# Two engines' loops over the turns of a relational graph stage, written out as straight code

## What is computed

```python
h = maximum(_layernorm(x), 0.0)
x = x + L0(h, edge_index, W_in, b_in, W_out, b_out)   # three rounds of normalised neighbour sums
h = maximum(_layernorm(x), 0.0)
# L1, the relational layer:
W_rel = einsum('rb,bio->rio', w_comp, weight)         # 64 relations from 16 bases
h_all = einsum('ni,rio->nro', h, W_rel)
msg = h_all[src, etypes] * norm
agg = segment_sum(msg, dst, num_segments=3125)
x = x + relu(agg + h_bias + h @ loop_weight)
```

## Time and profile before

| | |
|---|---|
| median of 3 runs | 1128.37 us (1128.1 to 1135.03) |
| the profiled execution | 1126.62 us |
| its span, first to last instruction | 1125.0 us |
| busy: PE / DVE / POOL / ACT | 890.1 / 812.3 / 555.3 / 358.3 us |
| the dearest group by busy time | L569, the gathers: 392.7 us |
| TensorE's mean granted clock over the span | 0.812 |

### The profile page before, as it was taken

One profiled execution on the slowest core, in us unless ns is written; L12 is line 12 of the kernel. 1 busy time (PEld: TensorE's weight loads), 2 busy tenths in 40 slices (PEclk: granted clock), 3 DMA queues, 4 the chain that ended last, 5 costly groups with the idle time before them and its releaser, 6 DMA issues.

```text
span 1125.0 us, 27667 instructions
## 1 busy us (share of the span) xinstructions
PE 890.1 (79%) x5568; PEld 596.5 (53%) x5569; DVE 812.3 (72%) x2477; ACT 358.3 (32%) x706; POOL 555.3 (49%) x581
## 2 busy tenths in 40 slices
PE   4777777777677769999982888988888888887666
PEld 3622222222223349999971666766665666565434
DVE  7799999999975545544451768777777878888544
ACT  0402344555565530000131445353443332221000
POOL 4055555555420000000015777777777777777773
PEclk9565555555555559999995999999999999999878
DMA  5013444565532220001139211111111111111113
GB/s 134 5 54 86 99 107 118 123 130 129 120 88 78 70 53 1 2 2 29 37 96 318 60 49 50 48 49 49 50 51 49 51 49 52 51 51 52 49 52 86
DMA packets 86977, 79.46 MB, mean 71 GB/s; under 512 B 33772, under 2 KB 73757, under 8 KB 86797
## 3 DMA queue, kind: packets, MB, share of 16 engines
q0 software_dynamic: 39504, 41.84, 14.7%
q1 hardware_dynamic: 47420, 36.97, 12.4%
HBM read 50.02 MB, written 8.09 MB: 52 GB/s over the span
## 4 chain that ended last, share of the span: by engine, by line
PE 30%; DVE 22%; issue 14%; DMA 14%; DVEq 8%; POOL 7%; ACT 2%; SPq 1%; POOLq 0%; ACTq 0%
PE ps L1036 13%; DVE ohbuf L746 9%; PE ps L1104 8%; DMA CT<-h_dram,src_col 8%; POOL CT L569 7%; PE ps L962 5%; DVE CT L859 4%; DMA CT<-stage 4%; DVEq L862 2%; DVE CT L862 2%; DVE ohbuf L743 2%; PE ps L1084 2%; DVEq L112 2%; DVEq L859 1%; DMA CT<-x 1%
## 5 line engine op out<-in xcount | busy, mean ns | idle before, releaser
L569 POOL DMA_INDIRECT CT<-h_dram,src_col x391 | 392.7, 1004 | 127.0 <-issue 97.5
L1104 PE MATMUL ps<-CT 128*128 128x256 f32 x1180 | 312.8, 414 | 77.6 <-DVE CT L862 39.3
L962 PE MATMUL ps<-ohbuf 128*128 128x400 bf16 x590 | 246.1, 510 | 89.8 <-DVE ohbuf L746 56.0
L1104 PEld LDWEIGHTS ps<-CT 128*128 128x128 f32 x1180 | 207.5, 196 | 177.5 <-issue 159.4
L862 DVE SCALAR_TENSOR_TENSOR CT<-iota,dlP,CT 128x256 f32<-128x256 int16 x590 | 286.4, 485 | 5.8
L859 DVE COPY CT<-CT 128x128 f32 x590 | 138.2, 234 | 140.2 <-PE ps L1104 68.0
L746 DVE TENSOR_SCALAR ohbuf<-iota,keys 128x400 bf16<-128x400 int16 x590 | 205.1, 386 | 0.0
L962 PEld LDWEIGHTS ps<-ohbuf 128*128 128x128 bf16 x590 | 63.0, 107 | 253.4 <-issue 226.2
L1243 ACT COPY CT<-ps 128x256 f32<-128x256 f32 x200 | 77.6, 388 | 330.9 <-PE ps L1104 327.2
L1184 ACT CAST stage<-ps 128x800 bf16<-128x800 f32 x100 | 82.5, 825 | 188.1 <-PE ps L962 169.8
L743 DVE TENSOR_TENSOR ohbuf<-iota,keys 128x640 bf16<-128x640 int16 x118 | 96.2, 815 | 38.4 <-PE ps L962 38.1
(11 more groups left out here) (164 smaller groups left out, 529.1 us busy)
## 6 DMA issues: line engine op xcount, KB each, us to landing
CT<-stage SPq DMA_DIRECT2D x200, 100.0 KB, 3.4
u<-edge_type POOLq DMA_DIRECT2D x48, 256.0 KB, 10.5
CT<-h_dram,src_col POOLq DMA_INDIRECT x391, 2.6
coef_dram<-coef_out POOLq DMA_DIRECT2D x49, 64.0 KB, 7.9
CT<-coef_dram SPq DMA_DIRECT2D x1, 3048.0 KB, 11.1
out<-CT SPq DMA_DIRECT2D x4, 256.0 KB
ohbuf<-x SPq DMA_DIRECT2D x3, 320.0 KB, 4.2
x_dram<-ohbuf SPq DMA_DIRECT2D x3, 320.0 KB, 2.4
```

The costliest lines, as they stand in the source:

```text
L569: pool.indirect_dma_start(out=gring[:, (j + 1) % GRING, :], out_offset=None, in_=h2_dram, in_offset=bass.IndirectOffsetOnAxis(ap=src_col[: ...
L962: pe.matmul(ps[:, ds(counted.place(counts[u][0], RING), 1), 0:LO], ohA[:, u, :], ohB[:, u, :], start=False, stop=True, skip_group_check=Tr ...
L1104: pe.matmul(ps[:, ds(summed.place(counts[u][0], RING), 1), 0:WIN * BASES], gpair[:, u, :], kpair[:, u, :, :].rearrange("p b d -> p (b d)") ...
```

## The change

VectorE's loop over turns 1 to 57 and TensorE's over turns 0 to 57 become Python loops, so that each turn's code stands once in the program with its number as a constant. The two alignments ahead of the loops go with them. Nothing else changes: the same operations in the same order on every engine.

```diff
@@ VectorE @@
             operands(0, first=True)
             dve.wait_ge(ld_coefs, 16)
-            dve.addr_align(BLOCK, offset=0, max_nops=0)
-            with dve.Fori(1, TURNS - 1) as c:
+            for c in range(1, TURNS - 1):
                 operands(c)
@@ TensorE @@
-            pe.addr_align(BLOCK, offset=0, max_nops=0)
-            with pe.Fori(0, TURNS - 1) as c:
+            for c in range(TURNS - 1):
                 sum_pairs(c)
                 complete_groups()
```

## The result

The changed kernel takes 1113.8 us (four runs, 1113.6 to 1114.0) where the kernel before takes 1129.9 (1128.1 to 1135.0): a ratio of 0.985, 95% interval 0.9815 to 0.9885. It is faster by 1.5%. The forecast was 1123, the range reached down to 1105.

| term | before, us | forecast | after, us |
|---|---|---|---|
| to the first gather | 599.7 | 599.7 | 597.9 |
| 390 gather periods | 510.5 (1.309 each) | 505.5 | 499.2 (1.280 each) |
| last gather and tail to the span's end | 14.8 | 14.6 | 14.9 |
| span | 1125.0 | 1119.8 | 1112.0 |

A forecast was written before the change was run, and what follows sets the result against it. GpSimd's gathers were taken as the bound: the profiled 1126.6 us, less 5 for shorter gathers and 0.2 in the tail, plus 0 for code, gave 1121.4; with the runs' median 1.8 higher, 1123. Range 1105 to 1138.

The forecast's parts named there:

- What bounds the kernel: GpSimd's 391 gathers, one every 1.309 us, none waiting for anything; VectorE and TensorE only consume what they fetch.
- (a): VectorE's loop written out: 1.2 us a turn, 68 us of VectorE's time, none of it on the path.
- (b): TensorE's loop written out: about 0.45 us a turn, 26 us of TensorE's time, also off the path.
- (c): GpSimd's gathers after about 900 us: VectorE's scalar_tensor_tensor lengthens fewer; 11.4 us at stake, 5 us taken as saved.
- R2: Rival, faster: gathers come clear of VectorE altogether, gaining 23 us, to 1105 us; chance 0.09.
- R3: Rival, slower: VectorE's written-out step locks on the harmful distance, hitting every gather; +24 us, 1152 us; chance 0.08.
- (d): The tail after the last gather: TensorE's loop end just before it goes, 0.2 us saved.
- (e): Fetching the added straight code on VectorE and TensorE: 38 more packets for TensorE, at a cost of 0.
- R1: Rival, slower: code arrives late on TensorE; 1201 us, or 1131 if only jumps crossing a block stall; chance 0.09.
- the sign named in the prediction: Sign of a wrong forecast by late code: TensorE's idle time "issue" of over 1 us between turns.
- no shift of 0.09 us would help: By the port rule alone, VectorE's scalar_tensor_tensor starting 0.09 us sooner saves gathers nothing: term 0, time 1128.

The follow-up runs named there:

- f4_ahead: Changed kernel with three more sequencer instructions on VectorE ahead of each two pairs, from waits always met; 1136.3 us, 1.007 of before.
- f6_psum: Changed kernel with the scalar_tensor_tensor's row of 0 to 15 read from PSUM instead of SBUF in turns 1 to 57; 1103.0 us, 0.977 of before.
- c0_before: The kernel before, unchanged, run again for a profile; 1131.9 us in its one run.
- c1_after: The changed kernel, unchanged, run again; 1115.2 us, 0.988 of before.

## Why the prediction was right or wrong

**What bounds the kernel** was right: gather after gather, before and after, and none that waits. A change that takes work from two engines that aren't the bound gave 1.5%, and it came through the bound's own instruction.

**(a) and (b), the two loops.** Two pairs on VectorE were forecast to go from 1.44 to 1.26 us and went to 1.21; the idle time for tiles was forecast at 70 us or more and is 61.5, and the wait for TensorE, which was to shrink, went from 56.2 to 51.0. TensorE's 26 us were not measured by themselves. That these gains aren't on the path held. I said of (a) that nothing of it is on the path: as a count of VectorE's time that is so, but VectorE's step is what drags the gathers.

**(c), the gather itself,** is the term that was mis-sized: 5 us forecast, 11.3 us measured (510.5 - 499.2). Its parts don't add up either: "some 190 gathers" after 900 us are 163 by the earlier trace rows (116 + 47), which makes 9.8 us at stake in place of 11.4. The mechanism was half seen. Right were the culprit (a scalar_tensor_tensor that starts a little ahead of a gather), that 0.34 us ahead does no harm, and the 0.70 us distance (0.68). The step that failed is the sentence "Before 900 us the engines meet at no fixed distance and I leave 1.31 to 1.33 us as it is". They met at a fixed distance for rows of gathers there, 0.15 to 0.17 us, in step at 1.43 us, and this stretch gave the larger part, 8.9 us. Behind 900 us, where I had put all 5 us, 2.4 were gained, and I put them down to the distance inside two pairs, which f4_ahead shows not to be what decides. That the range holds the result owes more to R2's bound than to the working of this term.

**R3** (the lock settles on the harmful distance) had the right mechanism at the wrong kernel. I asked whether a written-out step of 1.26 us could lock to a gather of 1.25 and not whether the loop's 1.44 did already. As I read the three cases, a lock needs VectorE's step to lie above the gather's own period, 1.25 us, and below its longest, 1.23 + 0.30: 1.43 locks (before), 1.49 locks (f4_ahead), 1.21 doesn't.

**R2** (no gather is hit) didn't come about through the change; f6_psum brought it about by other means, with about the saving that was worked out for it: 23 us forecast, 24.8 measured against before, with the loops written out too.

**(d), the tail,** was forecast 0.2 us shorter and came out 0.1 longer, 14.9 against 14.8: nothing. TensorE's low clock begins sooner, as said (granted 0.94 from 900 to 1050 us in place of 1.00), at no visible cost.

**(e) and R1, the code,** were right: 38 packets were forecast for TensorE and 38 came, another 35 came in the second queue, and no gather waited for it. TensorE's idle time that is put down to nothing, ahead of the pairs' weight loads, went from 159 us (up to 3.0 at once) to 139 (up to 2.6), so no late code shows there either; the sign named in the prediction, over 1 us of it, was there before the change.

**The start.** The first gather was 1.8 us earlier, which no step had. c0_before has it at 600.3 and c1_after at 597.6, f4_ahead at 599.2; among kernels that are the same up to there this scatters by as much, so I count it neither for nor against.

The Trainium skill ("SBUF — State Buffer", section on the two separate sides) has VectorE's operations with two SBUF inputs hold the port that they share with GpSimd. With the runs in hand: that the second SBUF input is the means is borne out by f6_psum, where one input went to PSUM and the stretching ended. The prediction read the rule so that any overlap should block the whole gather, and found it against the rows. Read with the ends of the instructions, they agree with a lock. A lengthened gather ends 0.81 to 0.82 us behind the end of the scalar_tensor_tensor ahead of it, whatever the distance: by the earlier trace rows 1055.35 - 1054.54, by c0_before 727.41 - 726.60, by f4_ahead 762.23 - 761.42. Over the traces of before, after, c0_before, c1_after and f4_ahead this holds for 632 of the 653 gathers over 1.0 us. An undisturbed gather takes 0.944 us, so by an estimate from these two it needs what the engines share some 0.13 us after its start, and stands until the other instruction is done. A scalar_tensor_tensor of 0.48 us that starts 0.35 us ahead or earlier is done by then: that is why the one 0.34 us ahead cost 0.01 and the one 0.39 us ahead, still running, nothing. One that starts less than about 0.1 us ahead mostly comes second, and is itself made longer (0.52 in place of 0.48 at 760.74, 0.54 in the mean of the 20 in before that start 0.08 to 0.10 us ahead). So "no shift of 0.09 us would help" doesn't follow from a lock: a start that is 0.09 us earlier saves 0.09 us.

## What to carry to other kernels

An engine that isn't the bound can still set the bound's pace: look whether the bound's instruction has one duration or several, and what the other engine starts just ahead of the long ones. When two engines that share something run at nearly the same period, the one that is a little faster can be held at the slower one's, so a gain on the slower one shows, and slowing it a little costs: here 1.5% gained and 2% lost, though VectorE had idle time to spare. To see the hold, compare the ends of the two instructions, not only their starts. The lasting cure is to take away what they share, here one input moved to PSUM, which together with the written-out code gave 25 us, where that code alone gave 14 to 16.

## What the runs showed of the hardware

- A gather's issue on GpSimd takes 0.94 us, and up to 1.21 if a scalar_tensor_tensor with two SBUF inputs starts 0.10 to 0.35 us ahead of it; the closer to 0.10, the longer: 1.06 at 0.23 us, 1.13 at 0.16 (c0_before), 1.19 at 0.10 (f4_ahead). It ends 0.81 to 0.82 us behind the end of that instruction. Under 0.1 us ahead it is mostly the scalar_tensor_tensor that is lengthened, to 0.52 or 0.54 us, and now and then the gather, by up to 0.29 (1.23 us).
- With one of the two inputs in PSUM neither is: 0.946 us in the mean for 391 gathers (f6_psum), and 481 ns for the scalar_tensor_tensor.
- Entrainment: in rows of up to four or five gathers GpSimd followed VectorE at 1.43 and at 1.49 us a gather without any semaphore between them holding it.
- In three of five groups of runs, on two of four chips, sequencer instructions of VectorE and TensorE stood still for about 0.7 us at a time, before was 20 to 22% slower (1357 to 1374 against 1128 us), and the consumers were the bound. VectorE's loop alone gave 1.8 and 1.1% there, by another way than on a plain chip. The cause is open. So is the share of each loop by itself on a plain chip: TensorE's alone was within the noise on a held-up one (0.998, 0.996 to 1.000), and f4_ahead says only that it doesn't outweigh a slower VectorE.
